# A retrieval and projection kernel: two bursts of W around tile 0's turn, another split of the sums, and the turns one half group later

## The chip, the cores and the metric

One NeuronCore of one Trainium2 chip. The metric is the device time of one execution in microseconds; the median over runs counts.

## What is computed

```
retrieved   = mean(item_embeddings[indices], axis=1)      # 512 users, 50 rows each, H = 512
fused_input = concatenate([user_rep, retrieved], axis=1)  # 512 x 1024
fused_rep   = fused_input @ W_fuse + b_fuse               # 512 x 512
logits      = fused_rep @ W_proj + b_proj                 # 512 x 12500
```

Indices run to 99,999 for most columns while the table has 12,500 rows; an index past the end reads the last row.

## The kernel before

**Tiles and groups.** Users are split into 4 tiles of 128, W_proj into 25 chunks of 500 columns (TILES, CHUNK). One group is one tile times one chunk: 4 parts of 128 along H, and for each part three matmuls, since both factors are held as a rounded high part and a low rest (f_hi, f_lo, w_hi, w_lo) and three of the four products are taken (L660). The first 8 chunks stay resident: tile 0 goes over all 8, then tile 1, 2 and 3. After that the other 17 chunks are streamed, four tiles each.

**Retrieval.** VectorE sorts each user's indices, so that those of the last row come last (sort, L414). Seventeen columns of the sorted list pass through a ring of 9 buffers (PASSING, RING): POOL issues one indirect gather of 128 rows for each (L267), called slots 0 to 16 of a tile here; rows past the table's inner part are skipped, so late slots move few bytes. The first column goes to a buffer of its own, home, and so do, added by the DMA, the columns behind slot 16 (the "lap" gather, placed before slot LAPS_AT). The last row counts by a share (add_last). VectorE adds a slot by a masked multiply and add into PSUM (add, L471). For tile 0 it adds slots 0 to 10 only (DVE_FIRST), then the share and home; TensorE sums slots 11 to 16 by matmuls with scaled identities that ScalarE made (kept, L619), the total ahead of slot 16. For tile 1, TensorE sums the last two (PE_LAST).

**A turn** brings a tile's sum, transposed, into PSUM (turn_sum, L623), ScalarE scales it (mean), TensorE multiplies it with the second half of W_fuse (fuse, L646) on top of the users' part, and ScalarE and VectorE split the result (fused_hi, fused_lo). Turns of tiles 1 to 3 stand in the middle of group 6 of the tile before, their fuse behind that group (halfway).

**W's way.** SP loads a chunk in two halves into one of the buffers "raws": chunks 0 to 3 have four of them, two of which (in early) become the bias rows' place later; the others alternate over the first two. ScalarE rounds the half (split_hi, L327) and VectorE subtracts (split_lo, L507). SP is one queue in program order: chunks 2 to 5 stand behind a wait for tile 0's slot 16, chunks 6 and 7 behind the split of 4 and 5, stores and bias loads follow.

**Order.** Every engine's order is written out by hand. ScalarE evacuates tile 0's groups (evacuate_first), whose bias comes through a matmul (L673), VectorE all others (L535). Three PSUM banks rotate between the groups, and a turn takes one of them.

## Time and profile before

| | |
|---|---|
| median of 3 runs | 338.95 us (338.04 to 339.5) |
| profiled execution, its time | 338.66 us |
| its span | 336.6 us |
| granted clock, mean | 0.988 |
| TensorE matmul busy | 318.3 us (95%) |
| VectorE busy | 184.9 us (55%) |
| ScalarE busy | 68.5 us (20%) |
| POOL busy | 82.3 us (24%) |
| DMA mean | 224 GB/s, 75.24 MB |

Times of rows are microseconds from the span's start, on one core. The engines are PE (TensorE; PEld its weight loads), DVE (VectorE), ACT (ScalarE), POOL and SP. Matmuls overlap, so the time between two starts tells more than the duration of one. A granted clock of 1.00 is 2.4 GHz, 0.50 is 1.2 GHz.

### The profile page before, as it was taken

Reading aid. Unit: us, or ns where it says so; the run is one execution under the profiler, and the core shown is the slowest. Engines: PE = TensorE matmul, PEld = TensorE weight load, DVE = VectorE, ACT = ScalarE, POOL = GpSimd, SP = SyncE. Lnnn points to the kernel's source line nnn. Section 1 sums busy time; section 2 is a strip of 40 time slices with the busy share of each in tenths; the row PEclk is TensorE's granted clock in tenths of the full one; section 3 lists DMA queues with packets and bytes.
Section 4 is the critical chain, followed back from the end, with each engine's and each line's share of the span. In section 5 each row is a group of like instructions: output and inputs, shape, how many; then the busy total and the mean of one; then the engine's idle time right before and its main releaser. Section 6 shows DMA issues by size and latency. Waiting matters only on the chain.

```text
span 336.6 us, 4239 instructions
## 1 busy us (share of the span) xinstructions
PE 318.3 (95%) x1464; PEld 260.9 (78%) x1464; DVE 184.9 (55%) x317; ACT 68.5 (20%) x102; POOL 82.3 (24%) x84
## 2 busy tenths in 40 slices
PE   4959998599999999999999999999999999999996
PEld 1429876498888898888888888888888888888884
DVE  5899598795678833625454444535354544435222
ACT  2330653530020024022022220222012221020000
POOL 4777778677777100000000000000000000000000
PEclk9996999999999999999999999999999999999999
DMA  7994998989997212786755776568757466442222
GB/s 277 363 396 93 414 383 246 323 270 402 376 338 210 96 62 98 176 333 248 213 162 216 230 243 185 176 249 244 201 161 249 181 213 213 161 166 99 91 91 91
DMA packets 33837, 75.24 MB, mean 224 GB/s; under 512 B 5686, under 2 KB 21830, under 8 KB 33824
## 3 DMA queue, kind: packets, MB, share of 16 engines
q1 hardware_dynamic: 26912, 60.11, 52.2%
q0 software_dynamic: 6336, 13.92, 12.6%
q10 hardware_dynamic: 576, 1.05, 0.8%
q8 instruction: 6, 0.10, 0.1%
q14 instruction: 7, 0.06, 0.1%
HBM read 55.47 MB, written 25.60 MB: 241 GB/s over the span
## 4 chain that ended last, share of the span: by engine, by line
PE 71%; DVE 0%; issue 0%
PE bank L660 69%; PE bank L646 2%; PE bank L636 0%; DVE total L471 0%; DVE out_sb L535 0%
## 5 line engine op out<-in xcount | busy, mean ns | idle before, releaser
L660 PE MATMUL bank<-w_hi,f_hi 128*128 (+1 forms) x400 | 155.8, 390 | 0.0
L660 PE MATMUL bank<-w_lo,f_hi 128*128 (+1 forms) x400 | 155.3, 388 | 0.0
L660 PE MATMUL bank<-w_hi,f_lo 128*128 (+1 forms) x400 | 155.1, 388 | 0.0
L535 DVE TENSOR_TENSOR out_sb<-bank,early 128x500 f32<-128x500 f32 x92 | 62.4, 678 | 128.1 <-PE bank L660 125.5
L660 PEld LDWEIGHTS bank<-w_hi,f_lo 128*128 128x128 f32 x400 | 75.1, 188 | 15.5
L660 PEld LDWEIGHTS bank<-w_hi,f_hi 128*128 128x128 f32 x400 | 75.2, 188 | 15.0
L660 PEld LDWEIGHTS bank<-w_lo,f_hi 128*128 128x128 f32 x400 | 75.2, 188 | 15.0
L327 ACT CAST w_hi<-w_raw 128x1000 fp32r<-128x1000 f32 x46 | 47.1, 1029 | 151.4 <-DMA w_raw<-w_proj 96.4
L267 POOL DMA_INDIRECT ring<-item_embeddings,rows x68 | 71.0, 1045 | 24.8 <-issue 16.6
L507 DVE TENSOR_TENSOR w_lo<-w_raw,w_hi 128x1000 fp32r<-128x1000 f32 (+1 forms) x58 | 55.4, 977 | 2.3 <-ACT w_hi L327 2.3
L471 DVE SCALAR_TENSOR_TENSOR bank<-ring,mask,bank 128x512 f32<-128x512 f32 x56 | 42.1, 752 | 4.5 <-DMA ring<-item_embeddings,rows 1.0
L613 PE MATMUL bank<-early 128*128 128x512 f32 x32 | 15.6, 644 | 5.0 <-DMA early<-w_fuse 5.0
L613 PEld LDWEIGHTS bank<-early 128*128 128x128 f32 x32 | 6.5, 210 | 12.5 <-issue 12.5
L646 PEld LDWEIGHTS bank<-ret_t,wf_ret 128*128 128x128 f32 x128 | 14.8, 192 | 0.9 <-issue 0.6
L646 PE MATMUL bank<-ret_t,wf_ret 128*128 128x128 f32 x128 | 15.0, 275 | 0.5 <-ACT ret_t L339 0.5
L619 PE MATMUL bank<-ret_t,ring 128*128 128x128 f32 x48 | 8.7, 363 | 6.4 <-DMA ring<-item_embeddings,rows 4.4
L619 PEld LDWEIGHTS bank<-ret_t,ring 128*128 128x128 f32 x48 | 8.4, 275 | 7.6 <-issue 7.6
L339 ACT ACTIVATE ret_t<-bank 128x128 f32<-128x128 f32 x16 | 3.1, 283 | 52.2 <-PE bank L636 38.4
L344 ACT ACTIVATE f_hi<-bank,bf_col 128x128 fp32r<-128x128 f32 x16 | 5.9, 368 | 9.5 <-PE bank L646 9.5
L520 DVE SCALAR_TENSOR_TENSOR f_lo<-bank,bf_col,f_hi 128x128 fp32r<-128x128 f32 x16 | 5.0, 347 | 4.8 <-ACT f_hi L344 4.8
L267 POOL DMA_INDIRECT home<-item_embeddings,lap_row x4 | 6.3, 1575 | 1.8 <-DMA home<-item_embeddings,rows 0.8
L673 PE MATMUL bank<-f_lo,f_hi 128*128 128x500 f32 x8 | 3.6, 446 | 3.1 <-ACT out_sb L357 3.0
(60 smaller groups left out, 61.6 us busy)
## 6 DMA issues: line engine op xcount, KB each, us to landing
logits<-out_sb SPq DMA_DIRECT2D x100, 250.0 KB, 2.6
w_raw<-w_proj SPq DMA_DIRECT2D x46, 500.0 KB, 6.9
early<-b_proj SPq DMA_DIRECT2D x25, 250.0 KB, 5.9
early<-w_proj SPq DMA_DIRECT2D x4, 500.0 KB, 6.7
ring<-item_embeddings,rows POOLq DMA_INDIRECT x68, 6.2
early<-user_t ACTq DMA_DIRECT2D x4, 256.0 KB, 4.1
early<-w_fuse SPq DMA_DIRECT2D x4, 256.0 KB, 5.4
wf_ret<-w_fuse SPq DMA_DIRECT2D x1, 1024.0 KB, 19.0
```

The lines of the kernel that those rows point to most:

```text
L267: return nc.gpsimd.indirect_dma_start(out=to, out_offset=None, in_=table, in_offset=bass.IndirectOffsetOnAxis(ap=column, axis=0), **how)
L327: nc.scalar.copy(w_hi[:, slot, 2 * h:2 * h + 2, :], raws[raw_of(c)][:, 2 * h:2 * h + 2, :])\
L344: nc.scalar.activation(f_hi[:, t, n, :], fused_ps[n][:, t * P:(t + 1) * P], ACT.Identity, bias=bf_col[:, n:n + 1]).then_inc(f_hi_ready, 1)
L471: nc.vector.scalar_tensor_tensor(total[:] if i == last_add(t) else total_ps[:], here, mask[:, t, i + 1:i + 2], total_ps[:], ALU.mult, ALU. ...
L507: m = nc.vector.tensor_tensor(w_lo[:, c % RESIDENT, k:k + step, :], raws[raw_of(c)][:, k:k + step, :], w_hi[:, c % RESIDENT, k:k + step, : ...
L520: nc.vector.scalar_tensor_tensor(f_lo[:, t, n, :], fused_ps[n][:, t * P:(t + 1) * P], bf_col[:, n:n + 1], f_hi[:, t, n, :].bitcast(F32), A ...
L535: nc.vector.tensor_tensor(out_sb[:, g % OUT_SLOTS, :], ps[:, 0:CHUNK], bias[:, c % BIAS_SLOTS, 0:CHUNK], ALU.add).then_inc(evacuated, 1)
L613: m = nc.tensor.matmul(fused_ps[n][:, :], wf_user[:, k, n * P:(n + 1) * P], user_t[:, k, :], start=(k == 0), stop=(k == HK - 1))
L619: m = nc.tensor.matmul(ps[:, k * P:(k + 1) * P], rows_in[:, k * P:(k + 1) * P], taken, start=(first and k == 0), stop=last, skip_group_che ...
L646: m = nc.tensor.matmul(fused_ps[n][:, t * P:(t + 1) * P], wf_ret[:, k, n * P:(n + 1) * P], ret_t[:, k, :], start=False, stop=(k == HK - 1) ...
L660: m = nc.tensor.matmul(ps[:, 0:CHUNK].unsqueeze(1), f[:, t, k, :], w, start=begin, stop=(f is f_lo and k == HK - 1))
L673: nc.tensor.matmul(group_bank(t, c)[:, 0:CHUNK], bias_pick[:, c:c + 1].to_broadcast([P, P]), bias_split, start=True, stop=False)
```

## The change

VectorE adds slots 0 to 13 of tile 0, TensorE sums 14 to 16; for tile 1 TensorE sums four (13 to 16) and VectorE's part then ends with the home rows. The lap gather goes one slot later. SP loads chunks 2 and 3 once slot 12 has landed and chunks 4 and 5 once tile 0's f_hi is complete; chunks 6 and 7 follow the first two stores and use the third and fourth raw buffer, so that the bias loads wait for their splits. ScalarE evacuates group 0 and 1 before it casts chunks 4 and 5. A turn's sum stands behind group 6, its fuse in the middle of group 7.

```diff
@@ -21,10 +21,11 @@
 SORTED = 24
 RING = 9
 HOME_AT = 8
-LAPS_AT = 13
-DVE_FIRST = 11
+LAPS_AT = 14
+DVE_FIRST = 14
 PE_FIRST = PASSING - DVE_FIRST
-PE_LAST = 2
+BURST_AT = 12
+PE_LAST = 4
 AHEAD = 5
 TURN_EVERY = RESIDENT + 1
 HOME_AFTER = 12
@@ -151,10 +152,10 @@
         first_evacuated = sem("first_evacuated")
 
         def raw_of(c):
-            return c if c < 4 else c % 2
+            return c % 4 if c < RESIDENT else c % 2
 
         def raw_uses(c):
-            return 1 if c < 4 else c // 2
+            return c // 4 + 1 if c < RESIDENT else (c - RESIDENT) // 2 + 3
 
         def place(t, i):
             return (PASSING * t + i) % RING
@@ -190,7 +191,7 @@
             def load_chunk(c):
                 for h in range(2):
                     if c >= 4:
-                        sp.wait_ge(lo_ready, 2 * (c - 4 if c < 6 else c - 2) + h + 1)
+                        sp.wait_ge(lo_ready, 2 * (c - 4 if c < RESIDENT + 2 else c - 2) + h + 1)
                     sp.dma_start(raws[raw_of(c)][:, 2 * h:2 * h + 2, :], w_proj[c, :, 2 * h:2 * h + 2, :])\
                       .then_inc(w_landed[raw_of(c)][h], 16)
 
@@ -221,17 +222,19 @@
             load_chunk(1)
             sp.dma_start(wf_ret[:], wf_dram[1]).then_inc(wf_ret_landed, 16)
             sp.wait_ge(user_fused, 1)
-            sp.wait_ge(slot_landed[place(0, PASSING - 1)], 16 * slot_uses(0, PASSING - 1))
-            for c in range(2, 6):
-                load_chunk(c)
+            sp.wait_ge(slot_landed[place(0, BURST_AT)], 16 * slot_uses(0, BURST_AT))
+            load_chunk(2)
+            load_chunk(3)
+            sp.wait_ge(f_hi_ready, HK)
+            load_chunk(4)
+            load_chunk(5)
             for c in range(RESIDENT):
+                store(0, c)
                 if c < 2:
                     load_chunk(c + 6)
-                store(0, c)
-                if c == RESIDENT - 3:
-                    sp.wait_ge(lo_ready, 8)
-                if c >= RESIDENT - 3:
-                    for b in range(3 * (c - RESIDENT + 3), min(3 * (c - RESIDENT + 4), BIAS_SLOTS)):
+                if c >= RESIDENT - 2:
+                    sp.wait_ge(lo_ready, 2 * c + 2)
+                    for b in range(4 * (c - RESIDENT + 2), 4 * (c - RESIDENT + 3)):
                         load_bias(b)
             for c in range(RESIDENT):
                 store(1, c)
@@ -375,16 +378,13 @@
             split_hi(2, (1,))
             split_hi(3)
             for c in range(RESIDENT):
-                if c < 2:
-                    split_hi(c + 4)
-                if c == RESIDENT - 2:
+                if c == RESIDENT - 1:
                     mean(1)
-                if c == RESIDENT - 1:
                     fused_hi(1)
                 evacuate_first(c)
                 if c < PE_LAST:
                     keep_last(c)
-                if c in (2, 3):
+                if c < 4:
                     split_hi(c + 4)
             for t in range(2, TILES):
                 mean(t)
@@ -454,6 +454,9 @@
                 dve.wait_ge(n_left_ready, 1)
                 dve.wait_ge(last_landed, 16)
 
+            def home_last(t):
+                return last_add(t) <= HOME_AFTER
+
             def add(t, i):
                 here = ring[:, place(t, i), :]
                 dve.wait_ge(slot_landed[place(t, i)], 16 * slot_uses(t, i))
@@ -466,9 +469,10 @@
                     dve.wait_ge(home_added, t + 1)
                 else:
                     dve.wait_ge(added, adds_done(t, i - 1))
-                if i == last_add(t):
+                final = i == last_add(t) and not home_last(t)
+                if final:
                     dve.wait_ge(ret_turned, t)
-                nc.vector.scalar_tensor_tensor(total[:] if i == last_add(t) else total_ps[:], here,
+                nc.vector.scalar_tensor_tensor(total[:] if final else total_ps[:], here,
                                                mask[:, t, i + 1:i + 2], total_ps[:], ALU.mult, ALU.add).then_inc(added, 1)
 
             def add_last(t):
@@ -478,8 +482,8 @@
                     nc.vector.scalar_tensor_tensor(total_ps[:], last_rows[:], share, total_ps[:], ALU.mult, ALU.add)\
                       .then_inc(last_added, 1)
                     return
-                if t == 1:
-                    dve.wait_ge(home_added, 1)
+                if t == 1 or home_last(t - 1):
+                    dve.wait_ge(home_added, t)
                 else:
                     dve.wait_ge(added, adds_done(t - 1, last_add(t - 1)))
                 nc.vector.tensor_scalar(total_ps[:], last_rows[:], share, None, ALU.mult).then_inc(last_added, 1)
@@ -497,7 +501,11 @@
                     nc.vector.tensor_copy(lap_row[:, t:t + 1], rows[:, t, bass.ds(lap + STATIC, 1)])\
                       .then_inc(lap_row_set[t], 1)
                 dve.wait_ge(home_landed[t], laps * 16)
-                nc.vector.tensor_tensor(total_ps[:] if t else total[:], total_ps[:], home[:], ALU.add).then_inc(home_added, 1)
+                final = t == 0 or home_last(t)
+                if t and final:
+                    dve.wait_ge(ret_turned, t)
+                nc.vector.tensor_tensor(total[:] if final else total_ps[:], total_ps[:], home[:], ALU.add)\
+                  .then_inc(home_added, 1)
 
             def split_lo(c, halves=(0, 1)):
                 for h in halves:
@@ -548,24 +556,21 @@
             sort(1)
             sort(2)
             sort(3)
-            for i in range(5):
+            for i in range(7):
                 add(0, i)
             count_columns()
-            bias_lo()
-            add(0, 5)
-            add(0, 6)
             split_lo(0, (0,))
             add(0, 7)
             add(0, 8)
+            bias_lo()
             split_lo(0, (1,))
-            add(0, 9)
-            add(0, 10)
+            for i in range(9, DVE_FIRST):
+                add(0, i)
             count_left()
             add_last(0)
-            split_lo(1, (0,))
             dve.wait_ge(laps_ready, 1)
             add_home(0)
-            split_lo(1, (1,))
+            split_lo(1)
             add_last(1)
             add(1, 0)
             fused_lo(0, (0, 1))
@@ -628,7 +633,7 @@
                         pe.wait_ge(kept_ready, PE_FIRST + j + 1)
                         pe.wait_ge(slot_landed[place(1, i)], 16 * slot_uses(1, i))
                         sum_in(ring[:, place(1, i), :], ret_t[:, j, :], first=(j == 0), ps=turn_bank(1))
-                    pe.wait_ge(added, adds_done(1, last_add(1)))
+                    pe.wait_ge(home_added, 2)
                     sum_in(total[:], ident[:], last=True, ps=turn_bank(1)).then_inc(ret_turned, 1)
                     return
                 pe.wait_ge(added, adds_done(t, PASSING - 1))
@@ -654,7 +659,7 @@
                     if first:
                         pe.wait_ge(f_ready, HK * t + k + 1)
                     if halfway is not None and k == HK // 2:
-                        turn_sum(halfway)
+                        fuse(halfway)
                     hi, lo = w_hi[:, bass.ds(slot, 1), k, :], w_lo[:, bass.ds(slot, 1), k, :]
                     for f, w, begin in ((f_hi, hi, k == 0 and not begun), (f_hi, lo, False), (f_lo, hi, False)):
                         m = nc.tensor.matmul(ps[:, 0:CHUNK].unsqueeze(1), f[:, t, k, :], w, start=begin,
@@ -701,10 +706,9 @@
             fuse(0)
             for t in range(TILES):
                 for c in range(RESIDENT):
-                    halfway = t + 1 if c == RESIDENT - 2 and t + 1 < TILES else None
-                    project_resident(t, c, halfway)
-                    if halfway is not None:
-                        fuse(halfway)
+                    project_resident(t, c, t + 1 if c == RESIDENT - 1 and t + 1 < TILES else None)
+                    if c == RESIDENT - 2 and t + 1 < TILES:
+                        turn_sum(t + 1)
 
             def stream(c, slot):
                 pe.wait_ge(lo_ready, 2 * (c + 1))
```

Three places in the engines' order. SP from the first burst on, before (names are tiles or semaphores; slot_landed7 is slot 16's):

```order
L194 DMA early<-w_proj 128x1000 [waits slot_landed7,user_fused]
L194 DMA early<-w_proj 128x1000 x3
L194 DMA w_raw<-w_proj 128x1000 [waits lo_ready] x6
L205 DMA logits<-out_sb 128x500 [waits first_evacuated]
L194 DMA w_raw<-w_proj 128x1000 [waits lo_ready] x2
L205 DMA logits<-out_sb 128x500 [waits first_evacuated] x5
```

and with the change (slot_landed3 is slot 12's):

```order
L195 DMA early<-w_proj 128x1000 [waits slot_landed3,user_fused]
L195 DMA early<-w_proj 128x1000 x3
L195 DMA w_raw<-w_proj 128x1000 [waits lo_ready,f_hi_ready]
L195 DMA w_raw<-w_proj 128x1000 [waits lo_ready] x3
L206 DMA logits<-out_sb 128x500 [waits first_evacuated]
L195 DMA early<-w_proj 128x1000 [waits lo_ready] x2
L206 DMA logits<-out_sb 128x500 [waits first_evacuated]
L195 DMA early<-w_proj 128x1000 [waits lo_ready] x2
```

The halves of chunks 2 and 3 wait for an earlier slot, those of 4 and 5 for f_hi, and those of 6 and 7 stand behind a store each.

VectorE from the count of columns to tile 0's home add, the difference (w_lo rows are the low splits of chunk 0 and 1):

```order
-L513 TENSOR_TENSOR f_lo<-total,f_lo 8x500
-L471 SCALAR_TENSOR_TENSOR bank<-ring,mask,bank 128x512 x2
-L507 TENSOR_TENSOR w_lo<-w_raw,w_hi 128x500 x2
-L471 SCALAR_TENSOR_TENSOR bank<-ring,mask,bank 128x512 x2
-L507 TENSOR_TENSOR w_lo<-w_raw,w_hi 128x500 x2
-L471 SCALAR_TENSOR_TENSOR bank<-ring,mask,bank 128x512 x2
+L515 TENSOR_TENSOR w_lo<-w_raw,w_hi 128x500 x2
+L475 SCALAR_TENSOR_TENSOR bank<-ring,mask,bank 128x512 x2
+L521 TENSOR_TENSOR f_lo<-total,f_lo 8x500
+L515 TENSOR_TENSOR w_lo<-w_raw,w_hi 128x500 x2
+L475 SCALAR_TENSOR_TENSOR bank<-ring,mask,bank 128x512 x5
```

Two further adds stand ahead of the count; the last run before the home rows has five adds instead of two.

TensorE at tile 1's turn with the change (before, the turn's rows stood between the two halves of group 6, with two slots):

```order
L624 MATMUL bank<-ret_t,ring 128x128 [waits slot_landed3,kept_ready,first_evacuated]
L624 MATMUL bank<-ret_t,ring 128x128 x3
L624 MATMUL bank<-ret_t,ring 128x128 [waits slot_landed4,kept_ready]
L624 MATMUL bank<-ret_t,ring 128x128 x3
L624 MATMUL bank<-ret_t,ring 128x128 [waits slot_landed5,kept_ready]
L624 MATMUL bank<-ret_t,ring 128x128 x3
L624 MATMUL bank<-ret_t,ring 128x128 [waits slot_landed6,kept_ready]
L624 MATMUL bank<-ret_t,ring 128x128 x3
L624 MATMUL bank<-ident,total 128x128 [waits home_added]
L624 MATMUL bank<-ident,total 128x128 x3
L678 MATMUL bank<-f_lo,f_hi 128x500 [waits first_evacuated]
```

Four slots and the total now stand between group 6 and the bias matmul of group 7.

## Rows read from the trace of the kernel before

**Rows 1.** The chain that ended last, in order of time: start us, us, what

```profile
92.29 0.76 DVE total L471
...
124.50 208.98 PE bank L660 x924
```

**Rows 2.** Timeline, TensorE: start us, us, engine line op out<-in xcount [idle before <-releaser]

```profile
25.73 6.71 PE L619 MATMUL bank<-ret_t,ring 128*128 128x128 f32 x32 [4.42 <-DMA ring<-item_embeddings,rows]
32.28 1.06 PE L619 MATMUL bank<-out_sb,ring 128*128 128x128 f32 x8
33.17 1.06 PE L619 MATMUL bank<-ident,total 128*128 128x128 f32 x8
...
35.58 3.81 PE L646 MATMUL bank<-ret_t,wf_ret 128*128 128x128 f32 x32 [0.46 <-ACT ret_t L339]
39.14 0.47 PE L673 MATMUL bank<-f_lo,f_hi 128*128 128x500 f32 x1
...
60.68 0.49 PE L673 MATMUL bank<-f_lo,f_hi 128*128 128x500 f32 x1 [1.64 <-ACT out_sb L357]
...
64.47 2.02 PE L619 MATMUL bank<-ret_t,ring 128*128 128x128 f32 x16 [1.94 <-issue]
...
72.08 0.47 PE L673 MATMUL bank<-f_lo,f_hi 128*128 128x500 f32 x1
...
98.49 0.47 PE L660 MATMUL bank<-w_hi,f_hi 128*128 128x500 f32 x1
```

**Rows 3.** Timeline, ScalarE, the high casts of W, 46 to 60 us

```profile
46.79 1.03 ACT L327 CAST w_hi<-w_raw 128x1000 fp32r<-128x1000 f32 x1 [1.43 <-DMA w_raw<-w_proj]
...
49.06 1.03 ACT L327 CAST w_hi<-w_raw 128x1000 fp32r<-128x1000 f32 x1 [0.47 <-DMA w_raw<-w_proj]
...
59.12 1.02 ACT L327 CAST w_hi<-w_raw 128x1000 fp32r<-128x1000 f32 x1 [4.58 <-DMA w_raw<-w_proj]
```

**Rows 4.** Stretches: us, busy of each engine, granted clock, DMA share, GB/s

```profile
25.50:28.00 2.50, 2.27 (x11) 2.30 (x11) 2.40 (x5) 0.00 (x0) 1.89 (x3) 0.50 0.60 112
...
30.00:32.00 2.00, 2.00 (x12) 2.00 (x12) 2.00 (x5) 0.00 (x0) 1.62 (x2) 0.55 0.11 19
...
34.00:49.00 15.00, 14.41 (x85) 12.33 (x84) 11.19 (x20) 8.82 (x16) 11.92 (x11) 1.00 1.03 415
```

**Rows 5.** Timeline, SP's issues of W

```profile
30.93 1.99 SPq L194 DMA_DIRECT2D early<-w_proj  x4
32.96 18.74 SPq L194 DMA_DIRECT2D w_raw<-w_proj  x6
```

**Rows 6.** Timeline, VectorE in tile 0's sum

```profile
15.87 3.35 DVE L471 SCALAR_TENSOR_TENSOR bank<-ring,mask,bank 128x512 f32<-128x512 f32 x4
...
22.92 1.27 DVE L507 TENSOR_TENSOR w_lo<-w_raw,w_hi 128x500 fp32r<-128x500 f32 x2
...
30.82 0.68 DVE L500 TENSOR_TENSOR total<-bank,home 128x512 f32<-128x512 f32 x1
```

**Rows 7.** Gathers into the ring issued in 20:24.5, 28.5:30 and 57:60, issue to landing

```profile
DMA to landing us min/median/max: 4.9/5.2/5.4
...
DMA to landing us min/median/max: 2.1/2.1/2.1
...
DMA to landing us min/median/max: 5.8/5.9/6.2
```

**Rows 8.** Timeline, POOL's gathers

```profile
21.46 1.00 POOL L267 DMA_INDIRECT ring<-item_embeddings,rows  x1 [0.30 <-issue]
...
28.77 1.00 POOL L267 DMA_INDIRECT ring<-item_embeddings,rows  x1 [0.30 <-DVE bank L471]
...
69.50 1.00 POOL L267 DMA_INDIRECT ring<-item_embeddings,rows  x1 [0.30 <-issue]
...
78.58 1.57 POOL L267 DMA_INDIRECT home<-item_embeddings,lap_row  x1 [0.31 <-issue]
```

**Rows 9.** Timeline, VectorE, tile 2's home rows

```profile
87.88 0.15 DVE L497 COPY lap_row<-rows 128x1 int32 x1 [2.24 <-DMA home<-item_embeddings,lap_row]
```

## The prediction

> **What bounds the kernel now.** First the chain of waits. It runs over TensorE nearly to the end: the last stretch alone is 924 matmuls in 208.98 us [rows 1], 0.226 us each, so a group of 12 costs 2.71 us and one of 13 (tile 0's, with the bias matmul) 2.94 us. Nothing can be won there. Ahead of it stand two things that the change touches: the turn of tile 2, where TensorE waited a moment for VectorE's total [rows 1], and everything before tile 1's first group.
>
> Then TensorE in order of time [rows 2]. Tile 0's first group begins at 39.14. Seven groups up to the one at 72.08 would take 20.6 us, tile 1's turn (three sums of 0.89 us, the distance of the rows at 32.28 and 33.17) 2.7 and its fuse 3.56 (35.58 to 39.14): 26.9 us. It took 32.94, so **about 6 us are stalls**, the row at 60.68 alone showing 1.64. The waits behind them are ScalarE's: its cast at 59.12 had waited 4.58 us for a W half [rows 3], and the evacuation behind it in program order released TensorE at 60.68.
>
> Then the DMA share by stretch [rows 4]: 415 GB/s from 34 to 49, but 112 and 19 GB/s around 26 to 32, because SP held chunk 2 until slot 16 had landed (30.93, [rows 5]). That hole is what the first burst fills. The same rows show a granted clock of 0.50, the 1.2 GHz level, after TensorE's idle time of 4.42 us [rows 2]: four slots took 6.44 us there (25.73 to the end before 32.28), 1.61 each against 0.89 at 2.4 GHz.
>
> **The change, part by part.**
>
> *Start of tile 0's groups.* VectorE does three adds more before the home rows. An add costs 0.86 us (3.35 us for four, [rows 6], whose distance is 0.865), so 2.5 us. Half a low split (1.2 of 1.27 us, [rows 6]) no longer stands ahead of the home add, but it also hid the loop's start, some 0.6 us by my estimate (0 and 1 are its ends; the loop's copy is such a row as the one at 87.88, [rows 9]). The home add ended at 31.5 (30.82 plus 0.68, [rows 6]); now 31.5 + 2.5 - 1.2 + 0.6 = 33.4. TensorE has slots 14 and 15 behind it by then (slot 16, issued at 28.77, landed 2.1 us later, and they are issued before it [rows 7, 8]). Left are the total and slot 16, two sums: 1.8 us at full clock, 3.2 at half.
>
> TensorE idled from 21.3 to 25.73 and now idles to about 29, when slot 14 lands (1.3 us a gather before slot 15 and 16, some 2.5 us to land), so I expect half clock when it starts. Before, it needed 6.1 us of work at 1.2 GHz until the clock came back near 31.8 [rows 4]. Slots 14, 15, total and 16 are 6.4 us of such work, but with a pause in front of the total. So slot 16 ends at 33.4 + 3.2 = 36.6 and the fuse starts at 37.1 (0.46 us for the first mean, [rows 2]). The fuse takes 3.56 us at full clock and 6.4 at half (32 passes at 0.201). I take 4.4, about a third of it at half clock: **groups start at 41.5 instead of 39.14, +2.4 us**. The ends are 40.2 (clock back before slot 16) and 43.6 (not before the fuse is over).
>
> On this the Trainium skill, "TensorE: Matmul & The Clock Gate", section "HAM oscillation — how this bites in real kernels", speaks against the change: waits for DMA between short stretches of matmuls let the clock fall, and each next stretch then starts slow, so work is better kept together. By that rule the sum would take the late end, 43.6; the 0.50 behind the 4.42 us wait agrees.
>
> *Gathers beside the burst.* The first burst (2 MB, issued at about 26.4 when slot 12 has landed, 4.9 us after 21.46 [rows 7, 8], and flowing some 2 us later, an estimate from the share of 0.11 that 30 to 32 still shows behind the issue at 30.93, so from 28.4 to 33.5 at 415 GB/s [rows 4, 5]) meets slots 15 and 16. Light gathers landed 2.1 us after issue in the hole and 5.9 us in a busy stretch [rows 7]. Slot 16 would then land between 31 and 34.7; it is wanted only at 35.0 at half clock, 34.3 at full. I cost it at nothing, at most 0.4 us.
>
> *W's supply.* Chunks 2 and 3 come 4.5 us earlier, but chunks 4 and 5 are issued at 42.0 (f_hi ready) instead of 32.96 [rows 5]. Halves arrive 2.3 us apart beside the gathers (casts at 46.79 and 49.06, [rows 3]); the first needs some 4.5 us from issue, those 2 us and its transfer. So chunk 4 is whole at 48.8, about 2 us later than before. Group 4 wants it at 41.5 + 11.8 = 53.3, so this is covered. Chunk 6 no longer waits for chunk 4's split but goes behind store 0, at about 46 instead of 50 to 51.5, and should land by 57 to 58 against 59.1. ScalarE evacuates before it casts, so groups 3 to 5 no longer hang on casts. **Such stalls as the 1.64 us go.** What is late next is VectorE: from the second half of chunk 2 until chunk 6 is split it has nine half splits (1.2 each) and ten adds (0.79): 18.7 us without a gap, ending 20.2 us after the first group. Group 6 starts with its first half, at +18.9 where a dense TensorE would want it at +17.6. So stalls shrink from 6 to 1.3 us.
>
> *Tile 1's turn.* Four slots and the total are 5 x 0.89 = 4.4 us, 1.8 more than before, all on TensorE's path. It ends at 41.5 + 18.9 + 2.9 + 4.4 = 67.7. Before: 64.47 + 2.67 = 67.1. So the gain on stalls (4.8) is nearly all paid back by the later start (2.4) and the two more sums (1.8); the order of fuse and half groups costs nothing in itself. On TensorE's path alone tile 1's first group starts at 67.7 + 2.9 + 3.6 = 74.2 against 75.0, and tile 2's at 74.2 + 8 x 2.71 + 0.44 + 3.56 = 99.9.
>
> *Tile 2's turn.* This is where I see the gain end. Gathers (2,5) and (2,6) now also wait for tile 1's turn, since slots 13 and 14 of tile 1 are TensorE's, and LAPS_AT puts one more gather ahead of the home lap. Before, (2,7) went at 69.50 and the lap seven gathers later at 78.58 [rows 8], 1.30 us each. Now ten gathers follow the turn: 67.7 + 13.0 = 80.7, 2.1 later. The lap's rows were taken up 9.3 us after its issue, VectorE having waited 2.24 us for them, at 87.88 [rows 9]; now 90.0. From there to the total's end is 5.17 us (92.29 plus 0.76, [rows 1]), so 95.2. Evacuating group 5 of tile 1, which group 7's bank now needs right behind the turn, comes after: 95.8. Group 7 with the fuse in its middle is 2.71 + 3.56, so tile 2 starts at **102.1**. Before: 98.49 + 2.71 = 101.2 [rows 2]. It is +0.9. The turn's place, half a group later, hides nothing of this since group 7 waits. Bounds for the lap: 6 us, the busy gather of [rows 7], takes it off the path; 9.3 keeps it there. I take 9.3, the same transfer in the same surroundings. Tile 3's turn I cost at nothing: no wait shows there in the chain before, and its new place gives it half a group, 1.36 us, more.
>
> **Sum.** 336.6 + 0.9 = 337.5 of span. The profiled execution was 338.66, the median of the runs 338.95; against the former, 339.6. That is no change by what a measurement of this kernel can tell, 0.5% or 1.7 us.
>
> **The rivals.**
>
> *TensorE's path decides (faster).* The lap lands within some 6 us and the clock is back before slot 16. Then groups start at 40.2, W comes 1.3 us sooner too, the turn ends near 66.0, and tile 2 starts at 66.0 + 32.2 = 98.2: minus 3.0, 336 us; with the clock as forecast 99.9, 337.4. For it: the lap's 9.3 us were in the stretch of W loads 8 and 9, which move too. Against: the same stretch moves by the same amount. 0.3.
>
> *The clock (slower).* The place is the fuse of tile 0. If the clock is not back before about 40, the groups start at 43.6, the turn of tile 1 ends at 69.8, and since VectorE's chain and POOL's ten gathers both hang behind it, tile 2 starts at 104.2: +3.0, 341.6. For it: TensorE idles longer and works in pieces. Against: its pieces add up to what sufficed before. 0.2.
>
> *W is late.* If the lap gather of tile 1 slows chunk 6 and 7 as it seems to have done with the load that landed at 59.1 [rows 3] and they land after 61, group 6 stalls 3 us: 342 or so. Their earlier issue speaks against it. 0.05.
>
> *The changed stage is hidden.* The first burst ends no stall, since chunks 2 and 3 never were late, and all gains come from ScalarE's order. This gives my time or a bit more and is inside the forecast, 0.45.
>
> **How the numbers follow.** Forecast, within 0.5%: 0.45. Faster by over 0.5%: 0.3, slower by over 0.5%: 0.25 (clock and late W). The range runs from the faster rival's 336.0 to 342.4, between clock and late W.
>
> **What would show it.** The first bias matmul near 41.5, with a granted clock of 0.5 until 37 to 39; DMA above 300 GB/s in 28 to 33 and low in 35 to 43; no idle time of TensorE over 0.5 us before group 6, then about 1 us; tile 1's turn ending near 67.7; the lap of tile 2 issued near 80.7 and VectorE's copy behind it waiting for the DMA; group 7 of tile 1 waiting for a total and an evacuation. Wrong if the groups start before 40.5, or if TensorE has no idle time between tile 1's first group and tile 2's: then the time is under 338.

## The result, and the profile after

| | before | after |
|---|---|---|
| median | 339.23 us (338.04 to 339.63, 4 runs) | 345.86 us (341.9 to 346.51, 4 runs) |
| ratio | | **1.0177**, 95% interval 1.0096 to 1.0258 |
| profiled execution, its span | 336.6 us | 343.9 us (its time 345.95) |
| granted clock, mean | 0.988 | 0.974 |
| start of tile 0's groups | 39.14 | 44.40 |
| end of tile 1's turn | 67.1 | 70.35 |
| start of tile 1's groups | 75.1 | 77.0 |
| start of tile 2's groups | 101.2 | 108.5 |

The change makes the kernel slower by 1.8%, with 1.0 to 2.6% as the interval; 339.6 us was forecast, in a range up to 342.4. The two spans differ by 7.3 us, and tile 2 starts 7.3 us later, so all of it is lost in the first 108 us. Three marks divide it: +5.3 at tile 0's first group, +1.9 at tile 1's first group (3.4 have been won back), +7.3 at tile 2 (5.4 are lost there). So the loss is made twice: ahead of tile 0, and between tile 1 and tile 2. (The end of tile 1's turn is no such mark: with the change, half a group more and two sums more lie ahead of it.) One of the four runs, 341.9, lies 4 us under the other three. It has no profile, so why it does stays open.

TensorE of the kernel after, from the first slot to the first group (timeline: start us, us, engine line op out<-in xcount, idle before and releaser), answers to [rows 2]:

```profile
34.22 3.75 PE L624 MATMUL bank<-ret_t,ring 128*128 128x128 f32 x16 [12.66 <-DMA ring<-item_embeddings,rows]
37.76 1.72 PE L624 MATMUL bank<-ident,total 128*128 128x128 f32 x8
39.32 1.06 PE L624 MATMUL bank<-ret_t,ring 128*128 128x128 f32 x8
40.84 3.81 PE L651 MATMUL bank<-ret_t,wf_ret 128*128 128x128 f32 x32 [0.46 <-ACT ret_t L342]
44.40 0.47 PE L678 MATMUL bank<-f_lo,f_hi 128*128 128x500 f32 x1
```

The first row is the loss: TensorE stood for 12.66 us, until a gather had landed. The total was not to blame; VectorE had it first, at 33.19 plus 0.69, forecast for 33.4. What happened to the gather stands on POOL and SP in the same stretch (timelines of the kernel after):

```profile
26.53 1.34 POOL L270 DMA_INDIRECT ring<-item_embeddings,rows  x1 [0.30 <-issue]
```

```profile
26.44 2.07 SPq L195 DMA_DIRECT2D early<-w_proj  x4
```

Slot 14's gather is issued at 26.53, 0.1 us behind the burst. Its landing time in the view by tile (ring, this one gather), and that of the same gather, issued at 26.46, in e1c, a kernel without the burst at this place (experiment 1):

```profile
DMA to landing us min/median/max: 7.6/7.6/7.6
...
DMA to landing us min/median/max: 3.4/3.4/3.4
```

The 2.1 us of [rows 7] are slot 16's in the kernel before, the lightest of the three; slots 14 and 15 landed there in 2.8 and 2.6 us.

The stretches show the rest (us, busy of PE, PEld, DVE, ACT, POOL, granted clock, DMA share, GB/s), against [rows 4]:

```profile
25.50:28.00 2.50, 0.00 (x0) 0.00 (x0) 2.37 (x5) 0.00 (x0) 2.06 (x2) 0.50 0.36 62
28.00:30.00 2.00, 0.00 (x0) 0.00 (x0) 1.79 (x3) 0.00 (x0) 1.52 (x2) 0.50 0.95 171
30.00:32.00 2.00, 0.00 (x0) 0.00 (x0) 1.79 (x6) 0.00 (x0) 1.47 (x2) 0.50 0.95 350
32.00:34.00 2.00, 0.00 (x0) 0.00 (x0) 1.31 (x4) 0.00 (x0) 1.61 (x2) 0.50 1.04 408
...
38.00:40.00 2.00, 2.00 (x15) 2.00 (x15) 0.00 (x0) 0.00 (x0) 1.52 (x2) 0.71 0.78 186
40.00:42.00 2.00, 1.54 (x14) 1.38 (x13) 0.00 (x0) 1.58 (x5) 1.56 (x2) 1.00 0.75 218
```

The hole of 19 GB/s is filled, as the change wants, and the gather is in the filling. The clock stays at 0.50, 1.2 GHz, while TensorE waits, and is back only in the stretch 38 to 40. Before, it was back near 31.8.

Behind the start TensorE runs as hoped. The bias matmuls of groups 0 to 6 are at 44.40, 47.44, 50.37, 53.32, 56.27, 59.21 and 62.14, 2.94 us apart, with no idle time; the stalls on ScalarE's casts ([rows 2], 60.68, and [rows 3], 59.12) are gone. One wait is left, in group 6:

```profile
63.17 0.49 PE L665 MATMUL bank<-w_hi,f_hi 128*128 128x500 f32 x1 [0.65 <-DVE w_lo L515]
...
94.59 0.49 PE L665 MATMUL bank<-w_hi,f_hi 128*128 128x500 f32 x1 [1.16 <-DVE out_sb L543]
...
98.28 0.63 PE L641 MATMUL bank<-ident,total 128*128 128x128 f32 x4 [0.73 <-DVE total L475]
...
100.70 0.79 PE L665 MATMUL bank<-w_hi,f_hi 128*128 128x500 f32 x1 [1.79 <-DVE out_sb L543]
```

The other three rows are the second loss, around tile 2's turn. What they wait for stands on VectorE (timeline, kernel after):

```profile
92.98 0.15 DVE L501 COPY lap_row<-rows 128x1 int32 x1 [2.64 <-DMA home<-item_embeddings,lap_row]
93.26 0.70 DVE L507 TENSOR_TENSOR bank<-bank,home 128x512 f32<-128x512 f32 x1
93.86 0.67 DVE L543 TENSOR_TENSOR out_sb<-bank,early 128x500 f32<-128x500 f32 x1
...
97.39 0.75 DVE L475 SCALAR_TENSOR_TENSOR total<-ring,mask,bank 128x512 f32<-128x512 f32 x1
99.97 0.68 DVE L543 TENSOR_TENSOR out_sb<-bank,early 128x500 f32<-128x500 f32 x1 [1.83 <-DMA logits<-out_sb]
```

The first two of TensorE's waits, 1.16 and 0.73 us, hang on the lap's rows: VectorE waited 2.64 us for them, and the evacuation at 93.86 and the total at 97.39 stand behind them in its order. The third, 1.79 us, hangs on a store, as the chain of waits says (start us, us, what):

```profile
88.62 11.27 DMA logits<-out_sb
...
99.97 0.69 DVE out_sb L543
```

A store of logits took 11.27 us, and its buffer was wanted for the evacuation of group 5. On SP's queue it stands behind chunks 8 and 9 of W (timeline, SP):

```profile
80.98 3.21 SPq L195 DMA_DIRECT2D w_raw<-w_proj  x2
84.23 0.83 SPq L206 DMA_DIRECT2D logits<-out_sb  x1
85.10 1.04 SPq L195 DMA_DIRECT2D w_raw<-w_proj  x2
88.62 8.38 SPq L206 DMA_DIRECT2D logits<-out_sb  x3
```

The median store of the profile's page lands in 2.7 us. The kernel before had the same wait of VectorE (timeline), but there it lay beside the fuse and TensorE did not stop for it:

```profile
94.49 0.68 DVE L535 TENSOR_TENSOR out_sb<-bank,early 128x500 f32<-128x500 f32 x1 [1.45 <-DMA logits<-out_sb]
```

TensorE's pauses cost the clock once more, which makes the 6 matmuls of the half group and the fuse's start slow (stretch, kernel after):

```profile
100.00:104.00 4.00, 3.30 (x9) 2.79 (x10) 3.79 (x6) 0.00 (x0) 3.08 (x4) 0.57 0.89 303
```

### The profile page after: what moved, and what is told of

Its sections match the earlier page's. It is cut to its first block, busy times and chain, and to the rows that moved or that the text cites. A ratio compares the mean times of both kernels' runs of the same rounds, so it can differ in the third digit from the quotient of the medians.

```text
span 343.9 us, 4227 instructions
## 1 busy us (share of the span) xinstructions
PE 318.3 (93%) x1456; PEld 260.9 (76%) x1456; DVE 186.3 (54%) x318; ACT 68.0 (20%) x101; POOL 81.5 (24%) x84
## 4 chain that ended last, share of the span: by engine, by line
PE 75%; DMA 10%; DVE 9%; issue 4%; POOL 1%; ACT 0%; POOLq 0%; DVEq 0%
PE bank L665 68%; DMA ring<-item_embeddings,rows 5%; DMA logits<-out_sb 3%; PE bank L651 3%; DVE bank L475 3%; PE bank L624 3%; DVE w_lo L515 2%; DMA home<-item_embeddings,rows 1%; POOL ring L270 1%; DVE key_left L419 1%; DMA out_sb<-indices 1%; DVE key_sorted L414 1%; DVE out_sb L543 1%; ACT w_hi L330 0%; DVE bank L464 0%
## 5 line engine op out<-in xcount | busy, mean ns | idle before, releaser
L270 POOL DMA_INDIRECT ring<-item_embeddings,rows x68 | 69.9, 1028 | 33.5 <-issue 16.9
L330 ACT CAST w_hi<-w_raw 128x1000 fp32r<-128x1000 f32 x42 | 43.0, 1030 | 141.2 <-DMA w_raw<-w_proj 136.4
L515 DVE TENSOR_TENSOR w_lo<-w_raw,w_hi 128x1000 fp32r<-128x1000 f32 (+1 forms) x50 | 50.3, 1024 | 0.0
L475 DVE SCALAR_TENSOR_TENSOR bank<-ring,mask,bank 128x512 f32<-128x512 f32 x58 | 43.6, 752 | 7.4 <-DMA ring<-item_embeddings,rows 3.8
L624 PE MATMUL bank<-ret_t,ring 128*128 128x128 f32 x56 | 8.5, 319 | 12.7 <-DMA ring<-item_embeddings,rows 12.7
L618 PEld LDWEIGHTS bank<-early 128*128 128x128 f32 x32 | 6.6, 211 | 12.7 <-issue 12.7
L515 DVE TENSOR_TENSOR w_lo<-early,w_hi 128x500 fp32r<-128x500 f32 x16 | 9.9, 671 | 0.6 <-ACT w_hi L330 0.6
L330 ACT CAST w_hi<-early 128x1000 fp32r<-128x1000 f32 x8 | 8.1, 1031 | 3.3 <-DMA early<-w_proj 3.3
```

Of the source, the lines that this page charges most:

```text
L270: return nc.gpsimd.indirect_dma_start(out=to, out_offset=None, in_=table, in_offset=bass.IndirectOffsetOnAxis(ap=column, axis=0), **how)
L330: nc.scalar.copy(w_hi[:, slot, 2 * h:2 * h + 2, :], raws[raw_of(c)][:, 2 * h:2 * h + 2, :])\
L475: nc.vector.scalar_tensor_tensor(total[:] if final else total_ps[:], here, mask[:, t, i + 1:i + 2], total_ps[:], ALU.mult, ALU.add).then_i ...
L515: m = nc.vector.tensor_tensor(w_lo[:, c % RESIDENT, k:k + step, :], raws[raw_of(c)][:, k:k + step, :], w_hi[:, c % RESIDENT, k:k + step, : ...
L618: m = nc.tensor.matmul(fused_ps[n][:, :], wf_user[:, k, n * P:(n + 1) * P], user_t[:, k, :], start=(k == 0), stop=(k == HK - 1))
L624: m = nc.tensor.matmul(ps[:, k * P:(k + 1) * P], rows_in[:, k * P:(k + 1) * P], taken, start=(first and k == 0), stop=last, skip_group_che ...
```

## The experiments

The theory is that the loss has two sources: **the burst** (the gathers of slots 14 to 16 are slowed by it) and **the store** (it stands behind chunks 8 and 9, and the new place of tile 2's turn exposes it). The rows above add to the second that the lap's gather runs beside the same loads. One rival is that the three adds more on VectorE, with the clock, make the late start by themselves; another that the new place of the turns costs it, whatever the store does.

Each measured beside the kernel before, in quiet periods, in which that kernel took 338 to 339 us:

| kernel | median us | kernel before | ratio, 95% | first group | tile 1 | tile 2 | span |
|---|---|---|---|---|---|---|---|
| before | | | | 39.14 | 75.1 | 101.2 | 336.6 |
| after | 345.86 | 339.23 | 1.0177 (1.0096 to 1.0258) | 44.40 | 77.0 | 108.5 | 343.9 |
| e1c: burst after slot 16 | 342.04 | 338.43 | 1.0126 (1.0057 to 1.0195) | 39.94 | 73.4 | 102.6 | 338.0 |
| e2c: turns back | 343.83 | 338.43 | 1.0141 (1.0112 to 1.0170) | 45.24 | 77.8 | 107.8 | 343.3 |
| e5c: chunks 8, 9 later | 340.32 | 337.81 | 1.0059 (1.0027 to 1.0092) | 43.82 | 76.4 | 102.7 | 338.1 |
| e3c: before, with the bursts | 341.02 | 337.81 | 1.0083 (1.0052 to 1.0115) | 42.81 | 77.7 | 103.9 | 339.3 |
| e6c: before, with the W order | 338.07 | 338.43 | 0.9999 (0.9974 to 1.0025) | 38.02 | 72.4 | 100.1 | 335.5 |
| e8: e6c and chunks 8, 9 later | 337.43 | 337.81 | 0.9977 (0.9950 to 1.0004) | 39.45 | 74.5 | 100.2 | 335.6 |

The ratios are those on record; they are not the quotients of the two medians, which give 1.0107 for e1c and 1.0160 for e2c. The last four columns are from the profiled execution of each; "tile 1" and "tile 2" are the starts of these tiles' groups. Tile 2's start is TensorE's last row before it plus what is left of group 7. Behind it every one of the eight executions takes 235.4 us (235.4 to 235.5), so the start of tile 2 is the whole story of each, and the two columns ahead of it say where it was made. A first group varies by itself: after, e2c and e5c have the same program up to it and begin at 44.40, 45.24 and 43.82, e6c and e8 at 38.02 and 39.45. So what is read from one execution's first group is good to some 1.4 us, no better.

**1. The first burst later** (from the kernel after):

```diff
-BURST_AT = 12
+BURST_AT = 16
```

> The changed kernel with its first burst behind slot 16, as e1, for a chip on which the kernel before takes about 339 us. Theory (the first burst holds back slots 14 to 16): tile 0's groups start near 41 instead of 44.4 and the time is 342 to 343 against 345.9 of the change. Rival (VectorE's longer sum sets the start): groups at 44, 345 to 346. Where the kernel before takes 355 us or more again, both: within 0.5% of it, as e1 and e1b.

TensorE and the stretches of this kernel (timeline, then us, busy of the engines, granted clock, DMA share, GB/s):

```profile
30.00 3.52 PE L624 MATMUL bank<-ret_t,ring 128*128 128x128 f32 x16 [8.07 <-DMA ring<-item_embeddings,rows]
33.87 1.16 PE L624 MATMUL bank<-ident,total 128*128 128x128 f32 x8 [0.35 <-DVE total L507]
34.86 1.06 PE L624 MATMUL bank<-ret_t,ring 128*128 128x128 f32 x8
36.38 3.81 PE L651 MATMUL bank<-ret_t,wf_ret 128*128 128x128 f32 x32 [0.46 <-ACT ret_t L342]
39.94 0.47 PE L678 MATMUL bank<-f_lo,f_hi 128*128 128x500 f32 x1
```

```profile
30.00:32.00 2.00, 2.00 (x9) 2.00 (x10) 1.79 (x6) 0.00 (x0) 1.41 (x2) 0.50 0.03 3
32.00:34.00 2.00, 1.65 (x10) 1.46 (x9) 1.31 (x4) 0.00 (x0) 1.68 (x2) 0.72 0.69 173
34.00:36.00 2.00, 1.92 (x16) 1.73 (x16) 2.00 (x4) 0.04 (x1) 1.55 (x2) 1.00 0.99 390
```

Nothing else is changed, and the first slot comes at 30.00 instead of 34.22, the first group at 39.94 instead of 44.40, as the theory had it. The three more adds stay in this kernel, so the rival's share is small: 39.94 against 39.14, 0.8 us for adds, clock and all, no more than two executions of one program differ by. Of the 5.3 us at the start 4.5 are the burst's. The clock came back in the stretch 32 to 34 here, 2 to 4 us after the work began, in the kernel after in 38 to 40, 4 to 6 after it; so 4.2 of the 4.5 us are the gathers' own delay.

The medians alone don't settle it: 1.0126 and 1.0177 overlap, and the profiled execution, 340.07, is the fastest of the four. The place of the loss is shown by the rows; its share of the median, 0.5% by these ratios, 5.9 us by the two spans, is not well measured. Of these 5.9 us, 4.5 are the start; from tile 1's first group to tile 2's this execution takes 29.2 us, against 31.5 with the change and 26.1 before. So the second loss is there, if smaller, and TensorE waits 1.16 us for the evacuation behind the store (chain of waits):

```profile
85.06 10.44 DMA logits<-out_sb
...
95.58 0.69 DVE out_sb L543
```

**2. The bursts alone** (in the kernel before):

```diff
-            sp.wait_ge(slot_landed[place(0, PASSING - 1)], 16 * slot_uses(0, PASSING - 1))
-            for c in range(2, 6):
-                load_chunk(c)
+            sp.wait_ge(slot_landed[place(0, 12)], 16 * slot_uses(0, 12))
+            load_chunk(2)
+            load_chunk(3)
+            sp.wait_ge(f_hi_ready, HK)
+            load_chunk(4)
+            load_chunk(5)
```

> The kernel before with the two bursts alone, as e3, where the kernel before takes 338 to 339 us. Theory: slot 16 lands 3 to 5 us later, groups start 2 to 4 us later, and W for chunks 4 to 7 comes 5 us or more later with ScalarE's old order: 342 to 345. Rival (a fuller DMA pays by itself): 337 to 338.5.

Timeline, TensorE of this kernel:

```profile
25.92 3.02 PE L622 MATMUL bank<-ret_t,ring 128*128 128x128 f32 x24 [3.32 <-DMA ring<-item_embeddings,rows]
31.51 2.04 PE L622 MATMUL bank<-ret_t,ring 128*128 128x128 f32 x8 [2.57 <-DMA ring<-item_embeddings,rows]
34.07 2.05 PE L622 MATMUL bank<-out_sb,ring 128*128 128x128 f32 x8 [0.51 <-DMA ring<-item_embeddings,rows]
...
42.81 0.47 PE L676 MATMUL bank<-f_lo,f_hi 128*128 128x500 f32 x1
```

With VectorE's share as it was, the burst makes waits for gathers here too, 2.57 and 0.51 us (the 3.32 us were 4.42 before). Slot 14's gather landed in 5.4 us although it was issued at 26.01, 0.3 us ahead of the burst, and slots 15 and 16 in 6.5 and 6.2. The first group is 3.7 us late and the kernel 0.8% slower, 341.02 us where 342 to 345 was expected, since 1.1 us are won back up to tile 1. The adds can't give this, for there are none more here. The burst's share stands in both directions.

**3. The turns back in the middle of group 6** (from the kernel after):

```diff
-                    project_resident(t, c, t + 1 if c == RESIDENT - 1 and t + 1 < TILES else None)
-                    if c == RESIDENT - 2 and t + 1 < TILES:
-                        turn_sum(t + 1)
+                    halfway = t + 1 if c == RESIDENT - 2 and t + 1 < TILES else None
+                    project_resident(t, c, halfway)
+                    if halfway is not None:
+                        fuse(halfway)
```

(and turn_sum in project_resident at half of the group, ScalarE's first mean at c == RESIDENT - 2).

> The changed kernel with the turns in the middle of group 6, as e2, for a chip on which the kernel before takes about 339 us. Theory (the turn behind group 6 exposes the evacuation of group 5, which waits for a store): tile 2 starts 3 to 4 us sooner, 342 to 343. Rival (the turns' place is neutral): 345 to 346. Where the kernel before takes 355 us or more: 0.5 to 0.7% faster than it, as e2 and e2b.

Neither the theory nor the rival came true: tile 2 starts 0.7 us sooner, not 3 to 4, and the 343.8 us lie between the two forecasts. It gives 1.0141 against 1.0177, with overlapping intervals, and the span is 0.6 us shorter, from a first group that is 0.8 later: the place of the turns by itself is worth 1.4 us or so here, and the other 4 of the second loss stay. In the trace the wait changes its name. TensorE no longer waits 1.79 us for an evacuation but longer for the total, which ends at 98.1 in both kernels (timeline, TensorE):

```profile
98.22 0.70 PE L642 MATMUL bank<-ident,total 128*128 128x128 f32 x4 [2.07 <-DVE total L476]
```

**4. Chunks 8 and 9 later** (from the kernel after), behind the stores of groups 3 and 5:

```diff
-                if c < 2:
-                    load_chunk(RESIDENT + c)
+                if c in (3, 5):
+                    load_chunk(RESIDENT + c // 4)
```

> The changed kernel with the loads of chunks 8 and 9 behind the stores of groups 3 and 5 of tile 1, as e5, where the kernel before takes 338 to 339 us. Theory (the store of group 2 of tile 1 took 11.3 us behind these loads and held group 7): the store lands in 3 to 5 us, TensorE's waits ahead of group 6 and 7 go, tile 2 starts 3 us sooner: 342 to 343 against 345.9. Rival (the store is late for another reason): 345 to 346.

SP and TensorE of this kernel (timelines):

```profile
80.00 12.46 SPq L206 DMA_DIRECT2D logits<-out_sb  x4
92.51 0.95 SPq L195 DMA_DIRECT2D w_raw<-w_proj  x2
```

```profile
95.85 0.63 PE L641 MATMUL bank<-ident,total 128*128 128x128 f32 x4 [0.30 <-DVE total L475]
```

That 0.30 us is all the idle time of TensorE between 63 and 104, where the kernel after has 3.7. Tile 2 starts at 102.7 instead of 108.5; the first group was 0.6 earlier by itself, so 5.2 us are due to these loads, more than the 3 us that were expected, and the time falls to 340.32 where 342 to 343 was expected. They act in two ways. The store of group 2 (issued at 87.0) lands in 4.2 us instead of 11.27, and the evacuation behind the total no longer waits: 2.0 us of TensorE's time. The lap's rows too are taken up sooner, 6.8 us after the gather's issue (83.79 to 90.55) instead of 8.6, and the total with them: 1.8 us. The rest, 1.4, is the clock, which does not fall again. The edit moves store and lap at once, so this division is read from the rows of two executions and not tested. The ratio goes from 1.0177 to 1.0059. What is left, +0.59%, still has the burst's late start in it.

**5. The W order alone** (in the kernel before: raw buffers, store 0 ahead of chunk 6, ScalarE evacuates ahead of its casts, bias loads later; no bursts, VectorE's share and the turns as before):

```diff
-                if c < 2:
-                    load_chunk(c + 6)
                 store(0, c)
+                if c < 2:
+                    load_chunk(c + 6)
...
-                if c in (2, 3):
+                if c < 4:
                     split_hi(c + 4)
```

> The kernel before with only the order of W behind tile 0's turn and ScalarE's evacuations changed, as e6, for a chip on which the kernel before takes about 339 us. Theory (this order is what removes the 6 us of stalls in tile 0): tile 1's turn ends 2 to 3 us sooner, 336 to 337. Rival (W's rate makes the stalls): 338 to 340.

Timeline, TensorE:

```profile
61.81 2.02 PE L616 MATMUL bank<-ret_t,ring 128*128 128x128 f32 x16 [2.97 <-ACT out_sb L356]
...
92.09 0.63 PE L633 MATMUL bank<-ident,total 128*128 128x128 f32 x4 [1.83 <-DVE total L468]
```

The turn ends at 64.5 instead of 67.1, 2.6 us sooner, of which 1.1 are an earlier first group. Counted from the first group, tile 1 begins after 34.4 us instead of 36.0: the order of W alone wins 1.6 us, not the 5.2 that the whole change wins there (3.4, and 1.8 for the two more sums). TensorE still waits 2.97 us for an evacuation ahead of the turn. Then it waits 1.83 us for tile 2's total, where it waited 0.25 before, because VectorE waits for the lap's rows (timelines, TensorE of the kernel before, VectorE of this one):

```profile
93.18 0.63 PE L636 MATMUL bank<-ident,total 128*128 128x128 f32 x4 [0.25 <-DVE total L471]
```

```profile
86.79 0.15 DVE L494 COPY lap_row<-rows 128x1 int32 x1 [3.82 <-DMA home<-item_embeddings,lap_row]
```

Tile 2 starts 1.1 us earlier, as much as the first group did, and the time is the same, 0.9999: what the order of W won is given back at this turn. The expected 336 to 337 us did not come; 338.07 lies where the rival had it.

**6. Both together** (e6c with the edit of 4).

> The kernel before with the order of W behind tile 0's turn (as e6) and the loads of chunks 8 and 9 behind the stores of groups 3 and 5 of tile 1. In e6c tile 1's turn ended 2.6 us sooner than before, but tile 2's total was only 1.1 us sooner, its home lap having landed beside chunks 8 and 9. Theory: with these loads away the lap lands in 5 to 6 us, TensorE does not wait at tile 2's turn, and the time is 335.5 to 336.5 where the kernel before takes 338.4. Rival (POOL's pace sets tile 2's total): as e6c, 338.

TensorE waits for nothing at tile 2's turn now (chain of waits):

```profile
71.93 20.39 PE bank L657 x90
92.32 0.44 PE bank L633 x4
```

But this is not because the total comes sooner, as the theory had it. The lap's gather, issued at 77.13, 1.5 us behind the first of four bias loads on SP, is taken up 9.2 us later; 5 to 6 was expected (timeline, VectorE):

```profile
86.30 0.15 DVE L494 COPY lap_row<-rows 128x1 int32 x1 [1.28 <-DMA home<-item_embeddings,lap_row]
```

The total's add starts at 90.98, against 91.20 in e6c. TensorE does not wait because it comes to the turn 2 us later, of which 1.4 are a later first group of this execution. So tile 2 starts at 100.2, as in e6c, and what the later loads would give an early start is not shown. The ratio, 0.9977 (0.9950 to 1.0004), is the best of all, and not told apart from the kernel before; 335.5 to 336.5 us was expected, 337.43 measured. A gain up to 0.5% is possible, none is shown.

**The same kernels in a disturbed period.** Twelve runs fell into a time in which the kernel before itself took 357.7 to 359.2 us instead of 338. Their ratios say little of the terms above, but they were made first and are told as they came.

| kernel | median us | kernel before | ratio, 95% |
|---|---|---|---|
| e1: burst after slot 16 | 359.0 | 359.24 | 0.9976 (0.9929 to 1.0022) |
| e1b: the same | 355.85 | 357.71 | 0.9960 (0.9921 to 1.0000) |
| e2: turns back | 357.37 | 359.24 | 0.9947 (0.9893 to 1.0001) |
| e2b: the same | 353.77 | 357.71 | 0.9934 (0.9881 to 0.9987) |
| e3: bursts alone | 357.44 | 359.24 | 0.9947 (0.9902 to 0.9992) |
| e3b: the same | 356.87 | 357.71 | 0.9953 (0.9909 to 0.9996) |
| e4: before, turns moved | 360.33 | 359.24 | 1.0036 (0.9995 to 1.0078) |
| e5: chunks 8, 9 later | 358.7 | 357.71 | 1.0000 (0.9952 to 1.0047) |
| e6: W order alone | 358.29 | 359.15 | 1.0036 (0.9984 to 1.0088) |
| e7: e1 and e2 together | 355.97 | 359.15 | 0.9948 (0.9892 to 1.0003) |
| b0: the kernel before | 359.96 | 359.15 | 0.9992 (0.9931 to 1.0052) |
| a0: the kernel after | 360.63 | 359.15 | 1.0045 (0.9980 to 1.0110) |

> The changed kernel with BURST_AT 16: chunks 2 and 3 are issued once slot 16 of tile 0 has landed, everything else as changed. Theory (the first burst holds back the light gathers of slots 14 to 16, which landed 7.6 us after issue beside it): slot 14 lands near 29.3, TensorE starts its slots about 5 us sooner, the home add at 33.9 ends the wait, tile 0's groups start near 41 instead of 44.4, and the time is 342 to 343 instead of 345.9. Rival (VectorE's three further adds set the start): the groups start at 44 and the time stays at 345 to 346.

> The changed kernel with the turns back in the middle of group 6 and the fuse behind it, all else as changed. Theory (behind group 6 the turn puts group 7 right behind the evacuation of group 5, which waits for a store of group 2 that takes 11 us): TensorE's wait of 1.79 us ahead of group 7 of tile 1 goes, tile 1's turn ends about 1.4 us sooner and POOL with it, tile 2 starts 3 to 4 us sooner, and the time is 342 to 343. Rival (the place of the turns is neutral and the loss is the late start of tile 0 alone): 345 to 346.

> The kernel before with one thing changed, SP's order of W: chunks 2 and 3 once slot 12 has landed, chunks 4 and 5 once tile 0's f_hi is complete. Theory: slots 14 to 16 land 3 to 5 us later, tile 0's groups start at 40.5 to 41.5 instead of 39.1, and since ScalarE still casts chunks 4 and 5 ahead of evacuating group 0, TensorE's stalls in tile 0 grow too: 342 to 344 against 339. Rival (the bursts help and the other parts cost): 337 to 338.5.

> The kernel before with only the turns moved: sum behind group 6, fuse in the middle of group 7. Theory: tile 1's first group starts about 1 us sooner, and at tile 2's turn this is given back, since group 7 now waits for the evacuation of group 5 (94.5 to 95.2 before, behind a store): 338.5 to 340 against 339. Rival (the new place is what costs by itself): over 341.

> The changed kernel with the loads of chunks 8 and 9 behind the stores of groups 3 and 5 of tile 1 instead of 0 and 1. Theory (the store of group 2 that held VectorE's evacuation of group 5 for 1.83 us was behind these 2 MB in SP's queue, and the home lap of tile 2 beside them): the store of group 2 lands in 3 to 5 us instead of 11, the wait ahead of group 7 goes, the lap lands within 5 to 7 us instead of 8.6, tile 2 starts 3 to 4 us sooner: 342 to 343. Rival (POOL's order alone makes tile 2 late): 344 to 346.

> The kernel before with only the order of W behind tile 0's turn changed: chunks 6 and 7 go behind the stores of groups 0 and 1 into the third and fourth raw buffer, the bias loads wait for their splits, ScalarE evacuates groups 0 and 1 before it casts chunks 4 and 5; one burst behind slot 16, sums, lap gather and turns as before. Theory (6 us of stalls in tile 0 come from this order, and only its gain is real): 2 to 3 us faster than the kernel before. Rival (the stalls come from the rate of W itself): within 1 us of it.

> The changed kernel with both suspects taken back: first burst behind slot 16 and turns in the middle of group 6. Theory: both losses go, and what is left is VectorE's longer sum (+2 us at the start), two more sums of TensorE (+1.8) against the stalls won (-5): within 1.5 us of the kernel before on either side. Rival (the longer sum of VectorE is a loss of its own): slower by 3 us or more.

> The kernel before itself, for its trace on a chip of these runs. On the first two chips it took 358 to 359 us instead of 339. If that is delay spread over all waits, its trace shows groups of tile 0 from about 45 (39.1 on the first chip) and TensorE without idle time behind tile 1's fuse as before.

> The changed kernel itself. Theory (its loss is made of the late slots 14 to 16 and of the store that group 7 waits for, on any chip): slower than the kernel before by 3 to 7 us here too. Rival (the loss is hidden where every gather is late anyway): within 2 us of it.

(e4 is the reverse of the diff under 3, made in the kernel before. e1b, e2b and e3b repeat e1, e2 and e3.)

One execution of a0 took 647.89 us and one of e7 816.02; nothing shows why. Here nothing is told to be slower than the kernel before, not even the kernel after (1.0045, interval over 1), which was expected to be 3 to 7 us slower here too, and what cost 0.8% in the quiet period, the bursts alone, now seems to gain 0.5%. The kernel before, profiled in this period, shows why it is no fair base (timelines, TensorE and ScalarE):

```profile
47.23 6.45 PE L646 MATMUL bank<-ret_t,wf_ret 128*128 128x128 f32 x32 [8.58 <-issue]
```

```profile
46.81 0.79 ACT L339 ACTIVATE ret_t<-bank 128x128 f32<-128x128 f32 x4 [23.90 <-remote]
```

Its last sum, begun at 37.59, was there by 38.7, and ScalarE took it up at 46.81; the groups began at 53.44 and not at 39.14. The same pause of 4 to 8 us stands in e3, e4 and e6 and not in a0, where the first group began at 47.71. No row names what ScalarE waited for, no experiment touched it, and its cause stays open. So of this period only this is drawn: the disturbance is of the size of the effects, and it does not fall on all kernels alike.

## Why the prediction was wrong

- **"Gathers beside the burst": wrong, the first step that failed.** It was costed at "nothing, at most 0.4 us". I took a light gather in a busy stretch at 5.9 us, from [rows 7], and let only slots 15 and 16 meet the burst, because I let it flow 2 us after its issue; then I had slot 16 wanted only at 35.0. In fact slot 14, issued 0.1 us behind it, met it too, and took 7.6 us instead of 3.4. The stretch 28 to 30 already moves 171 GB/s, with a DMA share of 0.95. Slot 14 is the first that TensorE wants, so the whole delay is on the path. e1c removes it (4.5 us of the start), e3c makes it in the kernel before (3.7 us). The mistake was above all which gathers I let meet the burst. The size was short as well: slots 15 and 16 took 6.9 and 6.3 us, so slot 16 landed at 35.8 and not by 34.7, which cost nothing since it was wanted only at 39.32.
- **The clock:** I had it fall and come back in the fuse. It was back when the fuse began, at 40.84: the fuse took 3.56 us, as at full clock. The rival "the clock" gave the side and under half of the size (+3.0 of 7.3), and by a mechanism that was not the one: TensorE was late because it had nothing to work on, not because it was slow. By the rule of the Trainium skill, "TensorE: Matmul & The Clock Gate", section "HAM oscillation — how this bites in real kernels", that waits for DMA between short stretches of matmuls make each next stretch start slow, the prediction had the late end, 43.6. It is nearest to the 44.40, but by luck: the trace agrees that the work after the wait starts at a granted clock of 0.50, and not that this made the groups late.
- **The adds, the home rows:** right. Forecast 33.4 for the home add's end, measured 33.9.
- **W's supply, the stalls, tile 1's turn:** right. No stall before group 6, there 0.65 us; from the first group to the turn's end 26.0 us, forecast 26.2. The prediction put this to ScalarE's order and W's; e6c, with these alone, wins 1.6 of the 5.2 us and keeps a stall of 2.97 us, and e3c, with the bursts alone, wins 1.1. Which parts together give the rest is not shown.
- **Tile 2's turn: right up to the total, then the second step that failed.** From the turn's end to the lap's gather 14.0 us (70.35 to 84.38), forecast 13.0; the lap's rows 8.6 us later, forecast 9.3; the total's end 5.2 after that, forecast 5.2. That gives the total at 98.1. Then I put the evacuation of group 5 right behind the total, 0.6 us. It began at 99.97, because its buffer waited for a store of 11.27 us. The trace of before had the same wait, 1.45 us at 94.49, and I passed it by since it then lay beside the fuse. With group 7 behind the turn nothing lies over it: "hides nothing of this" was my own sentence, on the total. The clock's fall at 100 to 104, some 1.4 us, was no term of this step either. That the loads of chunks 8 and 9 make the lap slow stood in the rival "TensorE's path decides" and was right: without them it took 6.8 us. e5c removes store, clock and part of the lap: 5.2 of 7.3 us, the only edit that is told from the kernel after by its interval (1.0059, up to 1.0092, against 1.0177, from 1.0096).
- The two sources add up to more than the loss (4.5 and 5.2 against 7.3) since the change also wins 3.4 us between them: 4.5 and 0.8 at the start, less 3.4, and 5.4 at tile 2's turn are 7.3.
- **Two small slips in the sum.** The four slots at half clock take 6.55 us from start to start (25.73 to 32.28), not 6.44. The early end, with the clock back before slot 16, comes out at 39.9 by the prediction's own terms (33.4, 1.6, 0.9, 0.46, 3.56), not 40.2. Neither changes the forecast.

The store behind 2 MB of loads fits what the Trainium skill, "DMA: Bandwidth & Descriptors", section "Queues, rings and completion order", says: each DMA engine takes the descriptors of one ring in their order, so those of a store behind loads on SP's queue come up behind the loads' own. The trace agrees: the last of these loads, issued at 85.7, landed 12.7 us later, at 98.4, and the store at 99.9. The same section has each DMA engine change between queues packet by packet. By that rule alone I would expect the gather on POOL's queue to pass between the burst's packets with little delay. The trace agrees only in part: it landed at 34.1, ahead of the burst's end at 37.3, but took 7.6 us instead of 3.4.

**What stays open:** the size of the first source in the medians; the 341.9 us run; how the 5.2 us of e5c divide between store and lap; whether e1c, e2c and e5c together would be faster than before (not tried in a quiet period, nor with e5 in the other; with tile 1's start of e1c and the stretch from there to tile 2 of e5c, tile 2 would start at 73.4 + 26.3 = 99.7, an estimate, against 101.2); and the disturbed period.

## What to carry to other kernels

Before a bulk load is moved into a hole of DMA traffic, list the small transfers that fall into the same hole and end a critical sum; start the load behind the last of them, or count their delay in full, the first one's above all. When a wait of TensorE is moved, look at what stands beside the work that used to cover it: an evacuation that waited for a store's buffer at no cost becomes the path. And a gain at one turn is only a gain if the next turn has no wait of its own: here the 1.6 us that the order of W won at tile 1 were paid back at tile 2.

## What the runs showed of the hardware that was not expected

- A gather for which few rows are taken lands in 2.1 to 3.4 us in a quiet stretch, in 5.9 beside steady traffic, in 7.6 when it is issued 0.1 us behind a burst of 2 MB of another queue, and still in 5.4 when it is issued 0.3 us ahead of it (e3c).
- A store of 250 KB took 11.27 and 10.44 us behind two pairs of half chunks on its own queue, and 4.2 with these loads away (e5c, where two stores ahead of it still took 8.5 and 7.2); the median of the page of the profile is 2.7.
- The time from the first sum to a granted clock of 2.4 GHz was not the same in three kernels: 2 to 4 us in e1c, 4 to 6 in the kernel after, and 6 before the change.
- The same kernel took 338 and 359 us in two periods, with one pause of 8 us on ScalarE in front of a sum that had been ready, and no row that names its cause.
